# Softmax weights of the window attention, spread by two engines instead of one

## The reference

```
x = x + attn_a(layernorm(x))
attn_a: qkv = h @ w_qkv.T + b_qkv; 16 heads of 16 features
        groups of 64 tokens; the first and the second 32 tokens of a group are windows of their own
        (the second ones rolled by one group and back, which leaves windows of 32 neighbours)
        out = softmax(q k^T / 4) v   in each window of 32 tokens and each head
```

## Time and profile before

| | us |
|---|---|
| median of three runs | 5856.6 |
| lowest and highest run | 5855.17, 5864.99 |
| the profiled execution | 5866.23 |
| its span, first to last instruction | 5864.5 |
| first stage, last of its TensorE instructions that turn values ends | 706.6 |
| TensorE, granted clock over the span | 0.970 |

### The profile page before, as it was taken

One profiled execution on the slowest core, in us unless ns is written; L12 is line 12 of the kernel. 1 busy time (PEld: TensorE's weight loads), 2 busy tenths in 40 slices (PEclk: granted clock), 3 DMA queues, 4 the chain that ended last, 5 costly groups with the idle time before them and its releaser, 6 DMA issues. The chain is left out here.

```text
span 5864.5 us, 131363 instructions
## 1 busy us (share of the span) xinstructions
PE 5415.1 (92%) x50016; PEld 3686.0 (63%) x50016; DVE 4478.5 (76%) x7377; ACT 3489.1 (59%) x5278; POOL 1553.5 (26%) x2076
## 2 busy tenths in 40 slices
PE   7888657999989979999999999999999997799999
PEld 5777546999978834444444444444444444699998
DVE  6888676555546678888888888888888886755554
ACT  4555453333325547878887888788888886433332
POOL 5666544333320000111111111111111113533332
PEclk9999878999989979999999999999999998899999
DMA  1111292222219921111111111111111112222221
GB/s 51 50 50 50 73 277 96 89 85 84 87 62 332 328 75 46 55 59 57 57 55 58 57 57 56 58 58 56 56 57 59 56 54 95 78 90 86 85 99 49
DMA packets 315520, 495.78 MB, mean 85 GB/s; under 512 B 36314, under 2 KB 221028, under 8 KB 311024
## 3 DMA queue, kind: packets, MB, share of 16 engines
q1 hardware_dynamic: 289736, 424.67, 22.8%
q0 software_dynamic: 24576, 64.56, 3.4%
q10 hardware_dynamic: 808, 1.07, 0.1%
HBM read 321.82 MB, written 168.82 MB: 84 GB/s over the span
## 5 line engine op out<-in xcount | busy, mean ns | idle before, releaser
L1752 DVE TENSOR_REDUCE at_best<-at_psM 128x2 f32<-128x1024 f32 x2048 | 2409.8, 1220 | 298.6 <-PE at_psM L1809 295.7
L1708 ACT ACTIVATE at_p<-at_psE 128x1024 f32<-128x1024 f32 (+1 forms) x2688 | 2080.0, 819 | 559.7 <-PE at_psE L1825 494.9
L1825 PE MATMUL at_psE<-at_q,at_k 50*128 50x512 f32 x4096 | 1097.7, 422 | 29.6 <-ACT at_p L1708 29.2
L1809 PE MATMUL at_psM<-at_k,at_q 48*128 48x512 f32 x4096 | 1026.1, 460 | 85.5 <-DVE at_best L1752 57.8
L1836 PE MATMUL at_psO<-at_p,at_v 128*17 128x256 f32 x16384 | 1087.1, 383 | 0.0
L1108 ACT ACTIVATE e_h_hi<-e_psH 128x512 fp32r<-128x512 f32 x512 | 305.7, 597 | 919.9 <-PE e_psH L90 771.4
L1182 DVE SCALAR_TENSOR_TENSOR e_h_lo<-e_psH,e_h_hi 128x512 fp32r<-128x512 f32 x512 | 353.8, 691 | 601.4 <-ACT e_h_hi L1108 529.1
L1809 PEld LDWEIGHTS at_psM<-at_k,at_q 48*128 48x128 f32 x4096 | 441.3, 186 | 482.8 <-DVE at_best L1752 290.5
L1836 PEld LDWEIGHTS at_psO<-at_p,at_v 128*17 128x17 f32 x16384 | 377.7, 97 | 557.4 <-issue 309.8
L1825 PEld LDWEIGHTS at_psE<-at_q,at_k 50*128 50x128 f32 x4096 | 522.7, 185 | 306.3 <-ACT at_p L1708 151.0
L90 PE MATMUL e_psE<-e_w_hi,e_h_hi 128*128 128x256 f32 x2048 | 583.0, 285 | 0.0
(11 more groups left out here) (210 smaller groups left out, 8400.3 us busy)
## 6 DMA issues: line engine op xcount, KB each, us to landing
e_w_raw<-in_w SPq DMA_DIRECT2D x64, 1024.0 KB
scratch_qk<-cp_qkh SPq DMA_DIRECT2D x64, 512.0 KB
scratch_qk<-cp_qkl SPq DMA_DIRECT2D x64, 512.0 KB
at_q<-scratch_qk SPq DMA_DIRECT2D x256, 128.0 KB
at_k<-scratch_qk SPq DMA_DIRECT2D x252, 128.0 KB
scratch_v<-cp_va SPq DMA_DIRECT2D x32, 544.0 KB
at_v<-scratch_v SPq DMA_DIRECT2D x126, 136.0 KB, 9.6
a_x<-in_x SPq DMA_DIRECT2D x32, 512.0 KB
```

The source lines that it names most:

```text
L1708: nc.scalar.activation(P[:, u:u + n, :], src, ACT.Exp, scale=HD ** -0.5).then_inc(p_ready, 1)
L1752: nc.vector.reduce_max(best[j % 2][:, h, :, qt], psM[h][:], AX_X).then_inc(m_taken, 1)
L1809: last = nc.tensor.matmul(psM[h][:, a, :], Q[j][r, 128 * qt:128 * qt + 128], K[j][r, 512 * h:512 * h + 512], start=True, stop=True)
L1825: last = nc.tensor.matmul(psE[:, u - u0 if n == 2 else 2, :], K[j][r, 128 * kc:128 * kc + 128], Q[j][r, 512 * half:512 * half + 512], star ...
```

## The change

Of the four copies of a tile into `PT`, that of partitions 96 to 127 is now made by ScalarE (`spread_last_rows`), with a semaphore of its own, `last_rows_ready`. GpSimd makes the other three, counts three instead of four on `pt_ready`, and waits once after the third. After the inverse deviation GpSimd has one new wait, for its own result. VectorE's transpose into `PC` and TensorE's value products wait for both semaphores.

```
--- before.py
+++ after.py
@@ -166,7 +166,7 @@
         xT_done, hi_ready, lo_ready = sem("xT_done"), sem("hi_ready"), sem("lo_ready")
         proj_done, proj_taken, keys_ready = sem("proj_done"), sem("proj_taken"), sem("keys_ready")
         s_done, s_shifted, p_ready, pc_ready = sem("s_done"), sem("s_shifted"), sem("p_ready"), sem("pc_ready")
-        pt_ready = sem("pt_ready")
+        pt_ready, last_rows_ready = sem("pt_ready"), sem("last_rows_ready")
         pv_done, oT_ready, turned = sem("pv_done"), sem("oT_ready"), sem("turned")
         o_ready, o_used, dve_seq, pool_seq = sem("o_ready"), sem("o_used"), sem("dve_seq"), sem("pool_seq")
         first_keys_ready = sem("first_keys_ready")
@@ -240,6 +240,8 @@
                 pool.wait_ge(var_ready, g + 1)
                 T.settle(pool)
                 nc.gpsimd.tensor_tensor(rstd[:], var_eps[:], exponent[:], ALU.pow).then_inc(rstd_ready, 1)
+                pool.wait_ge(rstd_ready, g + 1)
+                T.settle(pool)
 
             def spread_weights(n, b):
 
@@ -247,11 +249,11 @@
                 T.settle(pool)
                 after(pool, pv_done, n - 1)
                 T.settle(pool)
-                for w in range(4):
+                for w in range(3):
                     r = slice(32 * w, 32 * w + 32)
                     nc.gpsimd.tensor_copy(PT[b][r, :, r], PC[b][r, :, :]).then_inc(pt_ready, 1)
-                    pool.wait_ge(pt_ready, 4 * n + w + 1)
-                    T.settle(pool)
+                pool.wait_ge(pt_ready, 3 * n + 3)
+                T.settle(pool)
 
             def add_bias(g, s, i, t):
                 pool.wait_ge(o_ready, 4 * g + t + 1)
@@ -323,6 +325,12 @@
                 act.wait_ge(s_shifted, n + 1)
                 nc.scalar.activation(PR[b][:], PR[b][:], ACT.Exp, scale=HD ** -0.5).then_inc(p_ready, 1)
 
+            def spread_last_rows(n, b):
+
+                act.wait_ge(pc_ready, n + 1)
+                after(act, pv_done, n - 1)
+                nc.scalar.activation(PT[b][96:128, :, 96:128], PC[b][96:128, :, :], ACT.Copy).then_inc(last_rows_ready, 1)
+
             def take_values(n, b):
                 act.wait_ge(pv_done, n + 1)
                 after(act, turned, n - 1)
@@ -345,6 +353,8 @@
                     def keys(*heads):
                         if ahead:
                             spread_keys(g + 1, 1 - s, heads)
+                    if not (isinstance(g, int) and n < 1):
+                        spread_last_rows(n - 1, (t + 1) % 2)
                     if t == 0 and ahead:
                         split_hi(g + 1)
                     if t == 3:
@@ -369,6 +379,7 @@
                     if t == 2:
                         keys(3, 4)
             groups(act, NG, group)
+            spread_last_rows(4 * NG - 1, 1)
             take_values(4 * NG - 1, 1)
 
         @block.vector
@@ -429,7 +440,8 @@
 
             def weights_by_key(n, b):
                 dve.wait_ge(p_ready, n + 1)
-                after(dve, pt_ready, 4 * (n - 1))
+                after(dve, pt_ready, 3 * (n - 1))
+                after(dve, last_rows_ready, n - 1)
                 nc.vector.transpose(PC[b][:], PR[b][:]).then_inc(pc_ready, 1)
 
             def divide(n, b):
@@ -517,7 +529,8 @@
                 n = 4 * g + t
                 if t == 0:
                     pe.wait_ge(proj_taken, 8 * g + 8)
-                pe.wait_ge(pt_ready, 4 * n + 4)
+                pe.wait_ge(pt_ready, 3 * n + 3)
+                pe.wait_ge(last_rows_ready, n + 1)
                 after(pe, oT_ready, n)
                 for c in range(4):
                     for h in range(4):
```

## The result

The changed kernel takes 5817.0 us, median of four runs (5813.96 to 5818.46), where the kernel before takes 5856.4 on the same chip (5855.17 to 5864.99). The ratio is 0.9929, with an interval of 0.9916 to 0.9941: 39 us faster. Measured again on another chip it was 5818.0 against 5856.4, ratio 0.9930 (0.9917 to 0.9944).

A forecast was written before the change was run, and what follows sets the result against it. In the first stage TensorE, the engine with least room, waits for GpSimd's copies. Terms -43.4 + 1.6 + 4.2 + 1.9 = -35.7 us, taken from the median 5856.6, give 5821 us; range 5804 to 5846.

The forecast's parts named there:

- The wait for GpSimd's copies is what can be gained, and only in the first stage: First stage, TensorE's value products: all 43.4 us of waiting for GpSimd's spread weights goes; later stages keep their length.
- Three copies take at most 1.83 us, a gain of 1.08: GpSimd, per tile: three copies of 0.61 us without waits, where four with waits took 2.91 us.
- The copies end 0.65 us before TensorE is free: Tile 3 of each group: GpSimd's copies end at 518.75, TensorE is free at 519.40, so the wait goes whole.
- One semaphore more on TensorE: Before each tile's value products: one 0.06 us release on one tile of four, +1.9 us; bounds nothing to 7.7.
- The first projection would wait 0.13 us a group for the lower parts: TensorE after tile 3's values: a new wait for VectorE's lower parts in each of 32 groups, +4.2 us.
- The new wait for the deviation costs nothing: GpSimd before tile 2's copies: they start at most 0.5 us later, with only these copies waiting behind; cost nothing.
- ScalarE's copy takes 0.60 to 0.71 us and fits in the gaps: ScalarE, one added copy per tile: about 0.52 us of engine time, 0.05 late in step 0 per group, +1.6 us.
- The sum: First stage: -43.4 + 1.6 + 4.2 + 1.9 = -35.7 us, with each group 1.1 us shorter.
- The range from -43 to -20 us: Whole kernel: the mechanism's own range of gain, 5813 to 5837 us, extended to 5805 on the lower side.
- VectorE gets some room with fewer GpSimd copies: VectorE beside fewer GpSimd copies: some unpriced gain, the reason for extending the forecast down to 5805 us.
- The turns' waits unchanged near 30 us: Sign of being right: TensorE's turns still wait about 30 us for ScalarE's copy of the products.
- Slower if ScalarE's copy cost 1.24 us: Rival, ScalarE's gaps: above 1.24 us per copy the kernel slows; at 1.6, +42 us, 5899; chance 0.05.

The follow-up runs named there:

- e1: Kernel before, GpSimd still making all four copies but without waits between them, plus the new wait behind the deviation: 5840.7 us, ratio 0.9979.
- e2: Changed kernel with a wait after each of GpSimd's three copies and without the new wait behind the deviation: 5823.7 us, ratio 0.9943.
- e7b: Kernel before, with one projection moved ahead of the turn in TensorE's step 3: 5855.3 us, ratio 0.9998.
- e10: Kernel before, with only GpSimd's new wait for its own deviation result ahead of tile 2's copies: 5873.2 us, ratio 1.0027.
- e4: Changed kernel with one of GpSimd's three copies, the two middle windows' weights never written (timing only): 5817.5 us, ratio 0.9935.
- e3: Changed kernel with ScalarE copying the same 32 partitions twice, first into a spare tile: 5844.1 us, ratio 0.9981.

## Why the prediction was right

It said 5821, from 35.7 us; it was 5817, 39.4 by the medians and 38.6 by the stage. The mechanism was the one it named, and it had also named what would come next. The sizes in it were off in several places, and some of these cancel.

- *The wait for GpSimd's copies is what can be gained, and only in the first stage.* Right: e1, e2 and e7b show it. The listed wait fell by 33.7 us, not by all of 43.4: 0.2 is left in each group, 5.4 us between 100 and 650, and 4.3 at the two ends. I had expected under 5. The prediction read one group, with a wait of 1.16; the next one has 1.50, and only the mean of 1.28, which it took for the sum, covers both.
- *Three copies take at most 1.83 us, a gain of 1.08.* 1.93, a gain of 0.98. They start 0.66 us apart, not 0.57 to 0.61. The Trainium skill (GPSIMD Engine Reference, section 2.1 Instruction dispatch) says that each core goes on to the next instruction once its own share is done. The prediction drew from it that copies of different partitions could lie beside each other, and that is not what this trace shows: each starts 0.05 us after the one before has ended, though no two share a partition.
- *The copies end 0.65 us before TensorE is free.* They end 0.03 before. Of the difference 0.10 is the copies' length; 0.28 the start, which comes 0.33 us after the end of the transpose (493.24 + 0.70 = 493.94, copy at 494.27) where I had put 0.05; and 0.26 VectorE, whose transpose of tile 3 ends 0.76 us ahead of the next group's transposes and not 1.02 (its normalised tokens before it take 2.25 us, they had taken 2.00).
- *One semaphore more on TensorE: 0.06 us for one tile of four, 1.9 us.* The wrong size, and this is what is left of the wait. In the kernel before, and in e1, e7b and e10, the values start 0.05 or 0.06 us after the last copy every time they wait for it. With the second semaphore it is 0.24 in 27 of 32 waits of the changed kernel, and the same 0.24 in e2, where the copies wait for each other as before. That is 0.19 more in each steady group. ScalarE's copy, which that semaphore stands for, had ended long before (495.49). No run has the second semaphore without ScalarE's copy. On tiles 0 and 2 nothing was lost: from the scores to the values it is 4.00 and 0.60 us as before, within 0.01.
- *The first projection would wait 0.13 us a group for the lower parts, 4.2 us in all.* The list of waits hardly has it, but this is what bounds the group now. The prediction has the lower parts release the projection at 520.54, 2.67 us after the transposes (517.87); it is 2.79, with ScalarE's split 0.12 late. e4 shows that it stays at 2.78 when the copies are no longer waited for. So the 0.20 that the values lose lies inside this wait and costs nothing.
- *The new wait for the deviation costs nothing.* Right in the changed kernel, and only there: e10 puts it at 17 to 19 us in the kernel before. The prediction gave the reason that holds (only these copies wait behind it, and they have time), but it did not say what the wait would cost where that cover is gone.
- *ScalarE's copy takes 0.60 to 0.71 us and fits in the gaps.* The duration is 0.63. The engine's time is more than the 0.52 I took: from the key copy to the exponential it was 0.61 us and is 486.47 - 485.09 = 1.38, so 0.77. In step 0 the split starts 495.51 - 494.70 = 0.81 after the transposes of the next group, 0.69 before: 0.12 late for the 0.05 that I took, and this reaches the first projection: 3.7 us in 31 groups for the 1.6 that I booked.
- *The sum.* A group was to become 1.1 us shorter and became 1.14. I booked nothing for GpSimd's copies behind the change and 4.2 + 1.6 + 1.9 = 7.7 us for what comes after them. TensorE alone would have the first projection 519.40 + 1.01 - 517.87 = 2.54 us after the transposes; it is 2.79, and 0.25 x 31 is 7.7 us again. But it is made of other parts: 4 us are the lower parts, the rest is ScalarE's lateness, and nothing is the second semaphore, so that the 1.9 stood by luck for ScalarE's 2.1 too few. The copies' longer chain and the second semaphore, which used up the margin of 0.65 us and 0.2 more, did not show because the lower parts come last anyway. The range from -43 to -20 us was also narrower than its own bounds, which give -28 + 16.7 = -11 at the upper end.
- *VectorE gets some room with fewer GpSimd copies.* The opposite: its key and token operations became slower (last section).
- *The turns' waits unchanged near 30 us.* 24.4. The 28 waits of 0.20 at step 2 are gone from the list, but the turn starts 0.79 us after the scores where it was 0.86 (484.46 to 485.25, 507.55 to 508.41), so only 0.07 of each is real, 2 us in all. Why it is, no run shows.
- *Slower if ScalarE's copy cost 1.24 us.* That point lies too low. e3 has two copies, which take 484.37 - 482.47 - 0.61 = 1.29 us of the engine, and is still 12.6 us of stage faster than before. The formula took a gap of ScalarE for the slack of TensorE in every step; e3 lost in steps 3 and 0 alone.

## What to carry to other kernels

A handoff between engines is worth what the last chain into the waiting instruction loses, so follow that chain and not the busy shares. The same projection moved into the same idle gap of TensorE was worth 0.4 us of stage while GpSimd's chain was last, 2.2 once that chain had been shortened, and 10.7 together with two further edits. A wait that a list still shows need not cost anything: when another input of the next instruction comes as late, removing the wait moves it and gains nothing (e4). So check what the instruction behind it waits for, by the distance from a fixed point of the group. Before adding work to an engine, look at what its next instruction feeds and when that is wanted; in e3 the gap on the engine itself understated the room. And an added semaphore on the waiting engine is not free: here 0.19 us came with it.

## What was not expected of the hardware

GpSimd copies of 32 partitions x 512 elements start 0.66 us apart without waits and 0.77 with, so a wait of the engine for itself costs 0.11 us between copies. After the power (a row of 128 x 4 elements) the copies start 0.42 us after its end with the wait (e10) and 0.04 before its end without (511.84 + 1.19 = 513.03 and 512.99).

TensorE's second semaphore, already set, came with 0.19 us more between the end of the last copy and the values: 0.24 in 27 waits of the changed kernel, where it was 0.05 in all 34 before. In four of the five waits behind 650 us, at the end of the stage, it is 0.05 again; why, no run shows.

ScalarE's small copy costs 0.77 us of the engine behind a key copy, where it waits on two semaphores, though both are long set; in e3 the second of two, with no wait of its own, starts 0.54 after the first. That the waits make the difference is likely and not shown:

```profile
482.47 0.71 ACT L320 ACTIVATE a_kbd<-a_kT,a_quarter_mask 128x512 f32<-128x512 f32 x1
483.20 0.63 ACT L333 ACTIVATE a_spare<-a_pc 32x512 f32<-32x512 f32 x1
483.74 0.61 ACT L334 ACTIVATE a_pt<-a_pc 32x512 f32<-32x512 f32 x1
484.37 0.63 ACT L327 ACTIVATE a_p<-a_p 128x512 f32<-128x512 f32 x1
```

VectorE's key operations, which read and write SBUF, change their length with the GpSimd copies beside them. Before, after, and in e4 with one copy (busy us, mean ns):

```profile
L416 DVE TENSOR_SCALAR a_kbd<-a_kT,a_quarter_mask 128x512 f32<-128x512 f32 x128 | 68.6, 578 | 6.2 <-ACT a_kT L302 6.2
```
```profile
L427 DVE TENSOR_SCALAR a_kbd<-a_kT,a_quarter_mask 128x512 f32<-128x512 f32 x128 | 75.9, 634 | 5.9 <-ACT a_kT L304 5.9
```
```profile
L426 DVE TENSOR_SCALAR a_kbd<-a_kT,a_quarter_mask 128x512 f32<-128x512 f32 x128 | 55.1, 473 | 6.1 <-ACT a_kT L303 6.1
```

The key operation takes 473 ns with one copy a tile, 578 with four, 634 with three close together, and 685 in e2 with three that wait for each other; the token operation (L401) 505, 551, 608 and 537. So neither the number of copies nor their spacing alone sets this; it may be which copy meets which operation. VectorE's 15 us more in the changed kernel (68.6 to 75.9 and 62.8 to 70.2) stand in part in the chain of tile 3, the tokens' 0.25 us above; by e4 they cost nothing in the steady groups, as this chain was not the last. The Trainium skill, SBUF — State Buffer, section Who interferes with whom, says that a VectorE instruction in a two-port mode and a GpSimd instruction exclude each other for a whole instruction. The direction agrees with the 473 ns beside one copy and the 578 and more beside three and four; that it is this lock, no run here separates.
